# Causal attention in two passes: from group after group to one run of items, 22 items apart, on three rotating pairs of PSUM banks

## What is computed

```python
def _chunked_causal_attention(q, k, v):
    scores = q @ k^T / sqrt(8)          # per batch and head, 2048 x 2048
    scores = where(key <= query, scores, -inf)
    return softmax(scores) @ v
...
q, k, v = (x @ W.T as 16 heads of 8); out = attention(q, k, v); return out @ Wo.T
```

## Time and profile before

| | |
|---|---|
| median of three runs | 5901.07 us (5898.83 to 5901.5) |
| the profiled execution, its own time | 5908.11 us |
| span of its trace | 5906.1 us |
| granted TensorE clock, mean | 0.916 |
| TensorE matmul busy | 5179.1 us (88%) |
| VectorE busy | 3948.9 us (67%) |
| ScalarE busy | 2684.4 us (45%) |
| GpSimd busy | 2643.7 us (45%) |
| attention, from the first stack's landing to the last item's store | 3987.5 to 5267.1 us |

### The profile page before, as it was taken

One profiled execution on the slowest core, in us unless ns is written; L12 is line 12 of the kernel. 1 busy time (PEld: TensorE's weight loads), 2 busy tenths in 40 slices (PEclk: granted clock), 3 DMA queues, 4 the chain that ended last, 5 costly groups with the idle time before them and its releaser, 6 DMA issues.

```text
span 5906.1 us, 163733 instructions
## 1 busy us (share of the span) xinstructions
PE 5179.1 (88%) x71504; PEld 3133.2 (53%) x71696; DVE 3948.9 (67%) x5079; ACT 2684.4 (45%) x3457; POOL 2643.7 (45%) x947
## 2 busy tenths in 40 slices
PE   8899889988998899989998899867777887798999
PEld 5566556664666466646665566532222222246776
DVE  5988488956986588748983889437566666623333
ACT  1565445644665365535653556421444444451111
POOL 2888378845885488628881788310000000000000
PEclk7999899989999899989998999875888888888999
DMA  1111101110111011101111111020111000100000
GB/s 51 31 37 37 46 27 37 39 53 19 39 37 60 12 38 37 39 34 35 37 39 40 31 37 39 20 62 14 17 18 17 12 12 12 17 33 2 4 4 5
DMA packets 94224, 173.85 MB, mean 29 GB/s; under 512 B 23641, under 2 KB 35554, under 8 KB 91874
## 3 DMA queue, kind: packets, MB, share of 16 engines
q1 hardware_dynamic: 93538, 163.67, 10.6%
HBM read 55.71 MB, written 8.39 MB: 11 GB/s over the span
## 4 chain that ended last, share of the span: by engine, by line
PE 76%; DVE 8%; issue 5%; ACT 4%; DMA 3%; POOL 2%; SPq 1%; DVEq 0%; ACTq 0%; POOLq 0%
PE D L1127 7%; PE D L1046 6%; PE D L1061 5%; PE D L1068 5%; PE D L1191 4%; PE D L978 4%; PE D L1219 4%; PE D L1310 4%; PE D L1085 4%; PE D L1026 3%; PE D L1206 3%; PE D L1094 3%; PE D L1096 3%; PE D L1034 3%; DVE mxp L818 3%
## 5 line engine op out<-in xcount | busy, mean ns | idle before, releaser
L423 POOL TENSOR_TENSOR rn<-ss,mhalf 128x32 f32<-128x32 f32 x192 | 1212.2, 6313 | 314.3 <-DVE ss L711 312.2
L818 DVE TENSOR_REDUCE mxp<-D 128x1 f32<-128x512 f32 (+3 forms) x1280 | 722.2, 606 | 417.6 <-PE D L1194 268.9
L612 ACT ACTIVATE hh<-D 128x1024 f32<-128x1024 f32 (+1 forms) x320 | 283.8, 936 | 605.5 <-PE D L1209 477.0
L1127 PE MATMUL D<-PTb,V 64*64 64x32 f32 x24576 | 415.7, 222 | 60.2 <-issue 42.8
L769 DVE TENSOR_TENSOR TOK<-D,RA 128x1024 f32<-128x1024 f32 x384 | 466.4, 1215 | 0.0
L428 POOL TENSOR_TENSOR hh<-hh,rr 128x1024 f32<-128x1024 f32 x192 | 364.6, 1899 | 219.8 <-DVE rr L739 219.5
L432 POOL TENSOR_TENSOR XC<-XC,TOK 128x1024 f32<-128x1024 f32 x132 | 311.5, 2360 | 335.2 <-DVE TOK L769 335.0
L1127 PEld LDWEIGHTS D<-PTb,V 64*64 64x64 f32 x24576 | 396.7, 138 | 102.5 <-issue 102.1
L709 DVE TENSOR_REDUCE ss<-TOK 128x32 f32<-128x2048 f32 x192 | 436.9, 2276 | 1.1 <-POOL rn L423 1.1
L558 ACT ACTIVATE V<-D 128x512 f32<-128x512 f32 x384 | 229.3, 597 | 451.5 <-PE D L1094 384.7
L263 POOL TENSOR_TENSOR rstd<-var_s,mhalf 128x4 f32<-128x4 f32 x96 | 96.3, 1007 | 717.2 <-DVE var_s L238 717.2
(11 more groups left out here) (219 smaller groups left out, 10307.2 us busy)
## 6 DMA issues: line engine op xcount, KB each, us to landing
V<-V SPq DMA_DIRECT2D x936, 64.0 KB, 2.0
V<-V SPq DMA_DIRECT2D x192, 192.0 KB, 2.4
RA<-tabs_dram SPq DMA_DIRECT2D x6, 2048.0 KB, 7.8
RB<-watt_dram SPq DMA_DIRECT2D x6, 2048.0 KB, 12.2
parts_dram<-hh SPq DMA_DIRECT2D x48, 128.0 KB, 2.3
RA<-parts_dram SPq DMA_DIRECT2D x12, 384.0 KB
TOK<-parts_dram SPq DMA_DIRECT2D x36, 128.0 KB
RB<-parts_dram SPq DMA_DIRECT2D x12, 384.0 KB
```

What stands on the lines that cost most here:

```text
L423: pool.tensor_tensor(rn[:, st % 2, :], ss[:, :], mhalf[:, :], ALU.pow).then_inc(s["powed"], 1)
L612: act.activation(PTE[n % 2][:, 2 * half:2 * half + 2, 0:CH - r * P], ST2[half][:, :, 0:CH - r * P], ACT.Exp, scale=float(HD) ** -0.5)\
L818: dve.tensor_reduce(mxp[:, h, qt, kc:kc + 1], PB[2 + n % 2][:, 0:first_pass_keys(qt, kc)], AX.X, ALU.max).then_inc(s["max1"], 1)
L1127: m = pe.matmul(D01[64 * h:64 * h + 64, at:at + WIN], VW[n % 2][ks, (0 if r % 2 else 2) + h, p * DH:(p + 1) * DH], PTb[ks, p * P + 32 * r: ...
```

## The change

The 8 x 40 items become one list, `at` = 0 to 319 for the first pass and i = `at` - 22 for the second, in every engine's stream, written out without device loops.

- A first-pass item is now one (qt, kc) for four heads in two halves hp of two heads; a half fills a bank pair, and one `tensor_reduce` takes the maxima of both heads (2 x keys columns).
- The order on TensorE in one iteration is: scores of i for heads 0 and 1 (S0), first pass for heads 2 and 3 (F1), scores for heads 2 and 3 (S1), first pass for heads 0 and 1 (F0), then the values of item i - 1, then a turn of maxima or results where a chunk has ended three items before.
- The four halves take the bank pairs D01, D23, D67 in rotation; a half waits until the half three places ahead of it has been read (`released_by`).
- Maxima are finished by chunk of 512 queries (after items 4, 12, 24 and 40 of a group): one reduce on VectorE, seven small operations on GpSimd, one turn, one copy, and twelve transfers of 4 x 128 values on SyncE in place of three per group.
- Key stacks are loaded from ScalarE's stream (nine transfers, behind the exponentials of a group's third item), query stacks from SyncE's.
- The mask products of the second pass (L1209) go; GpSimd sets the masked exponentials to zero (`affine_select` on 4 x 128 columns of 16 of the 40 items of a group).
- The exponentials rotate over three buffers instead of two; the results are copied out by ScalarE, and the four divisions of a chunk are one instruction.

```diff
-        FIRST = [(h, qt, kc) for h in range(GH) for qt in range(NT) for kc in range(qt // 4 + 1)]
...
+        FIRST = [(qt, kc) for qt in range(NT) for kc in range(qt // 4 + 1)]
+        assert len(FIRST) == ITEMS
+        TOTAL = NG * ITEMS
+        LAG = 22
+        ENDS = [4, 12, 24, 40]
         def first_pass_keys(qt, kc):
             return min(CH, (qt + 1) * P - kc * CH)
+        def units_at(at):
+            return [(kind, at, hp) for kind, hp in (("S", 0), ("F", 1), ("S", 1), ("F", 0))
+                    if (at >= LAG if kind == "S" else at < TOTAL)]
+        UNITS = [u for at in range(TOTAL + LAG) for u in units_at(at)]
+        UNIT_NO = {u: m for m, u in enumerate(UNITS)}
+        def pair_of(unit):
+            return PAIR[UNIT_NO[unit] % 3]
+        def released_by(unit):
+            m = UNIT_NO[unit] - 3
+            if m < 0:
+                return None, 0
+            kind, at, hp = UNITS[m]
+            return ("exp2", 2 * (at - LAG) + hp + 1) if kind == "S" else ("max1", 2 * at + 2 - hp)
...
+        def chunk_end(at):
+            g, n = divmod(at, ITEMS)
+            return g * CB + ENDS.index(n + 1) if at >= 0 and g < NG and n + 1 in ENDS else None
...
+            def load_queries(g):
+                hg, p = divmod(g, 2)
+                if g >= 2:
+                    sp.wait_ge(s["pv2"], (g - 1) * ITEMS)
                 for rep in range(PARTS):
                     sp.dma_start(QST[p][rep * 24:(rep + 1) * 24, :].rearrange("r (h n) -> r h n", h=GH),
-                                 scr[0, p, bass.ds(hg * GH, GH)].rearrange("h s d n -> (s d) h n"))\
+                                 scr[0, p, hg * GH:(hg + 1) * GH].rearrange("h s d n -> (s d) h n"))\
                       .then_inc(s[f"stacks_in{p}"], 16)
...
-            def max_rows(p, g):
-                sp.wait_ge(s["neg_copied"], g + 1)
+            def max_rows(cg):
+                g, c = divmod(cg, CB)
+                sp.wait_ge(s["neg_copied"], cg + 1)
                 for part in range(PARTS):
-                    sp.dma_start(QST[p][KR + part:KR + part + 1, :].rearrange("r (x n) -> r x n", n=P),
-                                 nT[64 * (part % 2):64 * (part % 2) + 64, part // 2, :]).then_inc(s[f"neg_rows{p}"], 16)
...
+                    for h in range(GH):
+                        q0 = h * SEQ + c * CH
+                        sp.dma_start(QST[g % 2][KR + part:KR + part + 1, q0:q0 + CH].rearrange("r (x n) -> r x n", n=P),
+                                     nT[part * 16 + 4 * h:part * 16 + 4 * h + 4, cg % 2, :]).then_inc(s[f"neg_rows{cg % 2}"], 16)
+            load_queries(0)
+            load_queries(1)
+            for cg in range(CHUNKS):
+                max_rows(cg)
+                if cg % CB == 1 and cg // CB + 1 < NG and cg // CB >= 1:
+                    load_queries(cg // CB + 1)
+            sp.wait_ge(s["pv2"], TOTAL)
...
+            def mask_diagonal(i):
+                pool.wait_ge(s["exp2"], 2 * i + 2)
+                pool.affine_select(out=PTE[i % 3][:, :, 0:P], in_=PTE[i % 3][:, :, 0:P], compare_op=ALU.is_ge, fill=0.0, base=0,
+                                   pattern=[[0, GH], [1, P]], channel_multiplier=-1).then_inc(s["masked"], 1)
+            def split_max(cg):
+                pool.wait_ge(s["max_all"], cg + 1)
+                if cg >= 1:
+                    pool.wait_ge(s["neg_turned"], cg)
+                pool.tensor_scalar(nneg[:, :], mxa[:, :], -1.0, None, ALU.mult).then_inc(s["neg"], 1)
+                pool.wait_ge(s["neg"], cg + 1)
+                pool.tensor_copy(nhi[:, :], nneg[:, :]).then_inc(s["neg_hi"], 1)
+                pool.wait_ge(s["neg_hi"], cg + 1)
+                pool.tensor_tensor(nrest[:, :], nneg[:, :], nhi[:, :], ALU.subtract).then_inc(s["neg_rest"], 1)
+                pool.tensor_copy(nparts[:, 0, :], nhi[:, :])
+                pool.wait_ge(s["neg_rest"], cg + 1)
+                pool.tensor_copy(nmid[:, :], nrest[:, :]).then_inc(s["neg_mid"], 1)
+                pool.wait_ge(s["neg_mid"], cg + 1)
+                pool.tensor_copy(nparts[:, 1, :], nmid[:, :])
+                pool.tensor_tensor(nparts[:, 2, :], nrest[:, :], nmid[:, :], ALU.subtract).then_inc(s["neg_low"], 1)
+            gather_v(0)
+            for at in range(TOTAL + LAG):
+                if chunk_end(at - 1) is not None:
+                    split_max(chunk_end(at - 1))
+                if at >= LAG:
+                    i = at - LAG
+                    g, n = divmod(i, ITEMS)
+                    if n == 2 and g + 1 < NG:
+                        gather_v(g + 1)
+                    if ITEM[n][1] >= 4 * ITEM[n][0]:
+                        mask_diagonal(i)
...
+            def load_keys(g):
+                hg, p = divmod(g, 2)
+                if g >= 2:
+                    act.wait_ge(s["pv2"], (g - 1) * ITEMS)
+                for rep in range(PARTS):
+                    for r in range(PARTS):
+                        act.dma_start(KST[p][(rep * 3 + r) * 8:(rep * 3 + r + 1) * 8, :].rearrange("r (h n) -> r h n", h=GH),
+                                      scr[1, p, hg * GH:(hg + 1) * GH, rep].rearrange("h d n -> d h n"))\
+                           .then_inc(s[f"stacks_in{p}"], 16)
+            def exps(i):
+                g, n = divmod(i, ITEMS)
+                c, kt = ITEM[n]
+                r = max(0, kt - 4 * c)
+                if i >= 3:
+                    act.wait_ge(s["pv2"], i - 2)
+                for hp in range(2):
+                    act.wait_ge(s["score2"], 2 * i + hp + 1)
+                    act.activation(PTE[i % 3][:, 2 * hp:2 * hp + 2, 0:CH - r * P],
+                                   pair_of(("S", i + LAG, hp))[:, :].rearrange("p (h n) -> p h n", h=2)[:, :, 0:CH - r * P],
+                                   ACT.Exp, scale=float(HD) ** -0.5).then_inc(s["exp2"], 1)
+            def copy_o(cg):
+                g, c = divmod(cg, CB)
+                act.wait_ge(s["pv2"], g * ITEMS + ENDS[c])
+                if cg >= 1:
+                    act.wait_ge(s["o_turned"], cg)
+                act.activation(oTs, PB[4], ACT.Copy).then_inc(s["o_copied"], 1)
+            for p in range(2):
+                act.wait_ge(s[f"split_out{p}"], 16 * 6 * NC // 2)
+            act.wait_ge(s["ones_ready"], 2)
+            load_keys(0)
+            load_keys(1)
+            for at in range(TOTAL + LAG + 4):
+                if chunk_end(at - LAG - 2) is not None:
+                    copy_o(chunk_end(at - LAG - 2))
+                if 0 <= at - LAG < TOTAL:
+                    exps(at - LAG)
+                g, n = divmod(at - LAG, ITEMS)
+                if n == 2 and g >= 1 and g + 1 < NG:
+                    load_keys(g + 1)
...
+            def first_max(at, hp):
+                g, n = divmod(at, ITEMS)
+                qt, kc = FIRST[n]
+                keys = first_pass_keys(qt, kc)
+                dve.wait_ge(s["score1"], 2 * at + 2 - hp)
+                if g and kc == 0 and qt % 4 == 0:
+                    dve.wait_ge(s["max_all"], (g - 1) * CB + qt // 4 + 1)
+                dve.tensor_reduce(mxp[:, 2 * hp:2 * hp + 2, qt, kc],
+                                  pair_of(("F", at, hp))[:, :].rearrange("p (h n) -> p h n", h=2)[:, :, 0:keys], AX.X, ALU.max)\
+                   .then_inc(s["max1"], 1)
+            def chunk_max(cg):
+                g, c = divmod(cg, CB)
+                dve.wait_ge(s["max1"], 2 * (g * ITEMS + ENDS[c]))
+                if cg >= 1:
+                    dve.wait_ge(s["neg"], cg)
+                dve.tensor_reduce(mxa[:, :].rearrange("p (h j) -> p h j", h=GH), mxp[:, :, 4 * c:4 * c + 4, 0:c + 1], AX.X, ALU.max)\
+                   .then_inc(s["max_all"], 1)
...
+            def store_o(cg):
+                g, c = divmod(cg, CB)
+                hg, b = divmod(g, 2)
+                dve.wait_ge(s["o_turned"], cg + 1)
+                tv = PB[5].rearrange("p (b h x) -> p b h x", b=NBLK, h=GH)
                 dve.reciprocal(o_inv[:, :].rearrange("p (b h x) -> p b h x", b=NBLK, h=GH), tv[:, :, :, 8:9])\
                    .then_inc(s["o_inv"], 1)
...
+                dve.wait_ge(s["o_inv"], cg + 1)
+                dve.tensor_tensor(
+                    OTOK[:, b * NT + 4 * c:b * NT + 4 * c + 4, hg * 32:hg * 32 + 32].rearrange("p b (h d) -> p b h d", h=GH),
+                    tv[:, :, :, 0:8], o_inv[:, :].rearrange("p (b h) -> p b h", b=NBLK).unsqueeze(3).to_broadcast([P, NBLK, GH, 8]),
+                    ALU.mult).then_inc(s["o_stored"], 1)
+            for at in range(TOTAL + LAG + 4):
+                if at < TOTAL:
+                    first_max(at, 1)
+                    first_max(at, 0)
+                if chunk_end(at) is not None:
+                    chunk_max(chunk_end(at))
+                if chunk_end(at - 3) is not None:
+                    copy_max(chunk_end(at - 3))
+                if chunk_end(at - LAG - 3) is not None:
+                    store_o(chunk_end(at - LAG - 3))
...
+            def first_pass(at, hp):
```

(80 more changed lines are left out.)

223 lines of the change are left out of this document (35 added, 188 removed).

## The result

The changed kernel takes 5667.36 us, median of four runs (5660.95 to 5680.83), against 5901.28 (5898.83 to 5908.23) for the kernel before in the same comparison: ratio 0.9605, 95% interval 0.9585 to 0.9624. The range of 5590 to 5730 holds it, and the forecast of 5635 was 32 us too low. The profiled execution took 5660.95.

What follows compares the result with a forecast made beforehand. TensorE and VectorE nearly full within 123 us steps, plus 35 us boundaries. First load 5, head 44 + 3, items 900, keys 12, rows 6, tail 40 + 3: 1013 against 1279.6, 266 saved, hence 5635; range 5590 to 5730.

Steps and rivals of the forecast that it cites:

- the boundary's 245 us: Between attention steps: 35 us in which TensorE only turns results and maxima, seven times, would go.
- The item: Steady part: a full item takes 3.23 us, 0.43 of it F0's stall behind S0's exponential; 3.02 on average.
- Rivals B and C: Item's chain: B, 0.3 us longer, +90, 5725, chance 0.10; C, 0.25 shorter, 75 less, 5560, chance 0.06.
- The reduce over two banks: First pass on VectorE: a 1024-column reduce takes 1.22 us.
- The maxima rows: Last chunk's rows, turned after iteration 42, needed in 46: stall 0 to 2.7 us a group, 0.75 taken, 6 in all.
- The tail: End of attention: 22 second-pass items at ScalarE's pace, 40 us, and 3 for the last result.
- The key issues: Nine key transfers issued on ScalarE: 3.0 us, 2 of them reaching TensorE, six times, 12 in all.
- The select: GpSimd's masking of second-pass exponentials: 0.6 us, between 0.29 and 1.17, costing nothing; without cover up to 150 us.
- Rival A: Stalls at transfers, chunk 2's rows behind a query stack or slower ScalarE issues: +80, 5715, chance 0.15.
- Three of the prediction's own signs of being wrong: In the trace: scores waiting for `nT`, ScalarE's stream standing over 3 us at its issues, clock falling between items.
- Rival D: Steady part: F0's stall keeps TensorE's clock low, a full item 5.37 us, 5954 at half the items, chance 0.04.
- The two queues: Loads split over SyncE and ScalarE gain nothing; were two queues twice as fast, first load 13 us shorter.

Runs made afterwards that it cites:

- the rows in time: Maxima rows of a chunk sent in four transfers instead of twelve, against the changed kernel: 5632.63 us, ratio 0.9532.

## Why the prediction was right, and where it was off

- **What bounds the kernel, and the boundary's 245 us: right.** No stack wait is left behind the first, and with 36 items of distance it comes back at 12 to 15 us a group.
- **The item: right in its mechanism, 0.06 too short.** 3.29 against 3.23, with F0's wait on ScalarE in it, and shortened to 2.93 by shortening that chain alone. With the order or the pairs changed, the same way of adding up gave the full item to 0.06 (3.44, 3.23 and 3.87 us). ScalarE starts 0.70 behind S0 instead of the 0.64 read in step 8; over 298 items 0.06 is at most 18 us. Rivals B and C, 0.3 and 0.25 an item, fall with it.
- **The reduce over two banks** takes 1.224 us (1.22 forecast), read from the groups by form of the stage:

```profile
L897 DVE TENSOR_REDUCE mxp<-D 128x2 f32<-128x1024 f32 x447 | 540.7, 1224 | 172.4 <-PE D L1250 137.0 <-PE D L1254 17.6
```

- **The maxima rows: the step that failed.** The prediction had two bounds, 0.33 us an issue (copy, issues and landing 6.8 us, no stall) and 0.59 (9.9 us, a stall of 2.7), and took 0.75 us a group, 6 in all, since four rows are "nearer to the small stack issues". An issue takes 0.573:

```profile
L397 SPq DMA_DIRECT2D RA<-nT x192: 572/573/702, 3991.2 to 4854.7; - x192
```

  That is the upper of its two bounds (0.59, from the 64-row issues). The stall itself, 1.5 to 1.8 us in seven groups and 3.5 in the last, 14.3 in all, lies between the 0.75 chosen and the 2.7 of the upper bound, since the last transfer lands only 1.1 behind the last issue's end. What no term held is the low clock behind it, 21 us more. The two together are 35.4, where the sum had 6; that is 29 of the stage's 34. With four issues the stage is 1006.2, where the sum gave 1008, 6 of it for the rows.
- **The tail** is 57.2 instead of 43, 10.1 of it for the same reason (47.1 with the rows in time; the other 4 were not looked into). Here TensorE stands 3.5 us for the last rows, and the 20 us behind it have a clock of 0.57:

```profile
4969.88 7.34 SPq L397 DMA_DIRECT2D RB<-nT  x12
...
4978.29 1.89 PE L1270 MATMUL D<-RB,XC 75*128 75x512 bf16 x4 [3.47 <-DMA RB<-nT]
```

```profile
4975.00:4995.00 20.00, 16.71 (x64) 3.66 (x64) 0.55 (x2) 9.53 (x11) 0.00 (x0) 0.57 0.01 1
```

- **Costed too high.** The key issues hold ScalarE's stream for 3.09 us as forecast (3.0), but F0 waits 0.96 there instead of its usual 0.31, so 0.65 of the 2 us reach TensorE each time: 4 instead of 12. Taking them from ScalarE altogether gives 3.8 in the steady part. The head was 41.4 for 44. These, and smaller ones that I can't name singly, cover most of the 18 us of the longer item.
- **The select** takes 0.635 us, close to the 0.6 chosen between 0.29 and 1.17, and is hidden (0.2 us once). That it is the cover that hides it, the values ahead of S1 show: 31.4 us of waits.
- **Rival A** (transfers) came true in a small part: rows were late, but those of the last chunk and not of chunk 2, and no query stack stood in the way. Three of the prediction's own signs of being wrong appeared with it, each on a small scale: scores wait for `nT` (14.3 us), ScalarE's stream stands 3.09 us at its issues, and the clock falls behind these waits.
- **Rival D** (the clock) did not in the steady part of the changed kernel, 0.97, nor with the rows in time, 0.99 to 1.00, though F0 stands 0.31 in every item. It did in its rotation-less neighbour: 0.74, and 200 us slower than before. The prediction had it at 5954 for half of the items at the low clock, with an item of 5.4 (here 6.0, with one pair for both halves of the first pass), and gave it 0.04; the case lies one `pair_of` away. The Trainium skill, page "TensorE: Matmul & The Clock Gate", section "A second HAM failure mode: psum-queue depth-cycling", tells of it: banks cycled each iteration, short idle times between groups of products, and a clock that swings. The run with fixed pairs agrees (0.74); the kernel with the rows in time, which also cycles through its banks and idles in each item, does not (0.99), so the cycling alone doesn't bring it. What differs is that F0 stands 0.89 us instead of 0.31; that this brings the low clock was not shown by itself.
- **The two queues gained nothing**, as summed: the first load took 32.0 us with the keys on ScalarE and the queries on SyncE, 26.9 with all on SyncE, and 23.8 in the new kernel with all on SyncE in the order of the groups. The order and the queues were not changed one at a time. The Trainium skill, page "DMA: Bandwidth & Descriptors", section "Issuing engines are not separate DMA queues", holds that only issue time is saved; these numbers agree.

The split exponentials with four transfers, 5550.23, beat both kernels: 117 us below the changed one, some 350 below the one before.

## What to carry to other kernels

When a buffer pair rotates between engines, write down the occupation of one pair, product start to rewrite: it sets the item, and cutting the releasing instruction in two can be worth more than a better order (2.93 against 3.29 us here). Price a chain of small transfers by its issues, not by its bytes, and ask how far ahead of its need it starts: two items more of distance removed all 14.3 us of waiting. And price a short wait of TensorE with what the clock does behind it: here each microsecond of waiting for rows cost about one and a half more, and with fixed pairs the clock cost more than the waits. When two traces are compared stage by stage, set the start of a stage ahead of its first load: nearly half of what the keys on SyncE gained lay there.
